# A scan kernel on one core: Exp and Ln from one named table set, state sums two units behind, steps at other places, slot targets turned

## The chip, the core and the metric

One core of a Trainium2 chip. The metric is the device time of one execution in microseconds. The kernel is one hand-scheduled program: every engine runs its own instruction list in order, and semaphores are the only tie between them.

## The reference, cut

A vision tower over 64 images: 196 patches of 768 values and a class token make 197 tokens of 192 channels. One state-space layer, then a mixture of 8 experts:

```python
h = concat(cls_tok, patches @ W.T + b)
# layer 1 on layernorm(h)
xi, z = split(xn @ W_in); xc = silu(conv1d(xi, 4 taps) + conv_b)
Bm, Cm = split(xc @ W_x); delta = softplus(xc @ W_dt + b_dt)
s_t = exp(delta_t * A) * s_t-1 + (delta_t * x_t) * B_t   # 384 channels x 16 states, 197 steps
y_t = sum_states(s_t * C_t) + D * xc
h = h + layernorm((y * silu(z)) @ W_out) * gamma + beta
# layer 2: route each token of layernorm(h) to its best of 8 experts, with a capacity
h = h + prob_max * (expert(x) if kept else x)
```

## The kernel before, in words

**Pairs and units.** The main stage works on 32 pairs of images (`PAIRS`), 394 time steps side by side. A pair's scan is cut into 12 units (`UNITS`: 3 blocks of 128 channels, 4 groups of 4 states); a unit's states fill one of `BUFS` = 5 buffers `hb`. Each engine has a function `body(i, r, on)` with the pair's steps written out at places: k = 0 to 23 (two per unit) on VectorE and ScalarE, u = 0 to 11 on GpSimd and TensorE. `on` tells which neighbours of pair i have steps there: pair i scans (0), i+1 is being projected (1), i+2 is embedded (2), i-1 and i-2 are finished (-1, -2).

**Who does what.** Per unit, ScalarE writes two halves of `exp(delta*A)` into PSUM (`decays`, L703; two buffers, so `decays(k)` waits for scan k-2). VectorE makes `bx` (L1408) and two scans (L1419) in place. GpSimd multiplies by C (`times_c`, L514) and makes `bx` itself for units 5 and 9 (L521). TensorE spreads B for the next unit (`spread_b`, L1039; one bank, free when `bx` is done) and sums states (`state_sum`, L1050 and L1054), `LAG` = 3 units behind the scan. `take_y` (L1426) gates the sums of one block on VectorE.

Around it, for the other pairs: token product (`tok`, L986), `embed` (L1383) and `front_stats`, `front_norm` (L710), transposes (`front_t`, L996; copies L750 to L752), three `conv` products (L1005, L1007; copied at L771), `silu_x` (L800), `bc` and three `dt` products (L1014, L1023; copied at L776 to L783), the softplus (ScalarE: `Exp` L808, two roundings, `Ln` L822; GpSimd: `softplus_sum` L588, `softplus_rest` L594, `make_delta` L599, `make_du` L604), the z products and `silu_z` (L804), B and C split in three bf16 parts (`rest_bc` L527, `middle_bc` L792, `last_bc` L531, `third_bc` L796), C spread and copied (L1043, L757), then `out_product` (L1066), `copy_out` (L722), `out_squares` (L731), `rstd_out`, `out_norm`, `apply_gamma`, `add_residual` (L541, L547), `row_stats` (VectorE, k=1), `rstd` (GpSimd, u=0), `row_norm` (L710 too, ScalarE, k=3), `back_t`, `router`, `take_logits`.

**SyncE** issues the DMAs of body i in this order: patches of pair i+2 (L420), deltas of pair i, block 2 (L442), store of pair i+1's deltas (L433), their blocks 0 and 1, and last `store_rows(i-1)` (L427, L428), which waits for `row_norm(i-1)`. So the patches of pair i+2 are issued after `row_norm(i-2)`.

**Banks.** `ps_k2` are two PSUM banks through which all small products of a pair go in turn; `K_OF`, `OUT`, `TOKS`, `FT`, `BT`, `CS`, `ROUTE` give each product's number in that turn, and a product waits for the copy of the one two before it.

**Slot stage**, after the pairs: rank and target slot of each token (VectorE), then a product of one-hot matrices that turns targets into token ids by slot. 128 columns of 99 tokens go in 16 groups of 8: VectorE makes `lo_hot` (L1557) and 4 columns of `hi_hot` (L1561, L1563), ScalarE 4 (L924, L930, L931), TensorE multiplies (L1254). Then the expert tiles run, unchanged here.

**Table sets.** ScalarE's functions come in sets; a load (ACT_TABLE_LOAD) stands where the active set lacks the next function. In the text below a place is named by its k or u, and a pair's zero is the start of its second `bx`, `bx(1)`.

Of the kernel before, what the change touches and what calls it, by code (L numbers as in the profile page):

```python
# [19 lines left out]
I32 = mybir.dt.int32  # L20
BF16 = mybir.dt.bfloat16
U32 = mybir.dt.uint32
ALU = mybir.AluOpType
# [4 lines left out]
P = 128  # L28
# [6 lines left out]
H0 = 99  # L35
# [20 lines left out]
CLEARED = 6  # L56
# [4 lines left out]
GROUP = 8  # L61
GROUPS = COLS // GROUP
BY_DVE = GROUP // 2
# [9 lines left out]
LAG = 3  # L73
# [5 lines left out]
S_CONSTS = R_CONSTS + 11 + CLEARED  # L79
# [12 lines left out]
def build(nc, x, cls_tok, tok_w, tok_b, w_inx, w_zlo, w_zhi, conv_w, conv_b, w_x, w_dt, b_dt, a_log, d_skip, w_out, gamma,  # L92
# [4 lines left out]
    with ExitStack() as ctx:  # L97
# [95 lines left out]
        at[0] = ob_at  # L193
        assert CLEARED * 4 * DIM <= at[0]
        lo_hot = [carve(H0, GROUP, P) for _ in range(2)]
        hi_hot = [carve(H0, GROUP, 2, SC) for _ in range(2)]
# [9 lines left out]
        exv, prob, rsum, vmax, absent, rank_t, destf, dlo, dhi, idw, iota, one_cols, dhin, probn, idp = (carve(H0, COLS) for _ in range(15))  # L206
        hot_abs = [carve(H0, GROUP - BY_DVE, SC) for _ in range(2)]
        desti, dlo_i, dhi_i = (carve(H0, COLS).bitcast(I32) for _ in range(3))
# [49 lines left out]
        ps_s = pb[5]  # L258
        ps_t = pb[7]
# [86 lines left out]
        s_hotid = sem("ids_by_one_hot_ready")  # L346
        s_hotabs = sem("one_hot_distances_ready")
# [29 lines left out]
        K_OF = (20, 22, 21, 0, 2, 3, 1, 11, 15, 12)  # L377
        MADE = (1, 3, 2, 4, 6, 7, 5, 8, 10, 9)
        TAKEN = (1, 3, 2, 4, 6, 7, 5, 8, 10, 9)
        OUT, TOKS, FT = (4, 9), (6, 7), (16, 17)  # L380
        BT, CS, ROUTE = (13, 14), (8, 10, 18, 5), 19
# [101 lines left out]
        def _(pool):  # L483
# [80 lines left out]
            def slot_consts():  # L564
# [3 lines left out]
                pool.iota(idw.rearrange("p (b f) -> p b f", f=2), [[L, IMAGES], [HSTEP, 2]], base=-NOBODY, channel_multiplier=1,  # L568
                          allow_small_or_imprecise_dtypes=True).then_inc(s_pool1, 1)
                pool.iota(idp.rearrange("p (b f) -> p b f", f=2), [[-L, IMAGES], [-HSTEP, 2]], base=NOBODY, channel_multiplier=-1,  # L570
# [35 lines left out]
            def body(i, r, on):  # L606
                o = 1 - r
                for u in range(UNITS):
                    if 1 in on and u == 2:
                        rest_bc(i + 1, o)  # L610
# [4 lines left out]
                    if -1 in on and u == 8:  # L615
                        rstd_out(i - 1)
                    if -1 in on and u == 10:
                        apply_gamma(i - 1)
# [8 lines left out]
                    if 1 in on and u == 2:  # L627
                        last_bc(i + 1, o)
                    if 1 in on and u == 3:
                        softplus_sum(i + 1)  # L630
# [1099 lines left out]
```

## Time and profile before

| | us |
|---|---|
| median of 3 runs | 2980.11 (2979.86 to 2989.61) |
| the profiled execution | 2973.0 |
| its span | 2971.3 |
| busy: TensorE, VectorE, ScalarE, GpSimd | 2483.1, 2292.0, 2095.8, 2346.7 |
| mean granted TensorE clock | 0.938 of full |

Busy time is a union of an engine's instructions and says nothing about which of them is waited for. The span has three stages: the pairs until about 2300 us, routing and slots until about 2447, the expert tiles until the end. Each stage has its own bound, so the rows are read by stage.

### The profile page before, as it was taken

To read this page: it belongs to the slowest core of one execution; us is meant where nothing else is said; L and a number is where in the kernel's file an instruction comes from. 1 tells how busy PE (TensorE), PEld (TensorE's weight loads), DVE (VectorE), ACT (ScalarE), POOL (GpSimd) and SP (SyncE) were. 2 spreads that over 40 slices of the span, in tenths; PEclk is the share of its full clock that TensorE was granted. 3 is DMA by queue.
4 is the path that set the end of the run, shared out by engine and by line. 5 is a ranking of instruction groups with operands and counts; after the bars stand their busy time and mean duration, and the time that the engine had idled before them with its cause. 6 is when DMAs were issued, how large, how long until landed. Compare 5 with 4: busy or idle time off the path is not lost.

```text
span 2971.3 us, 38064 instructions
## 1 busy us (share of the span) xinstructions
PE 2483.1 (84%) x12650; PEld 1565.3 (53%) x12650; DVE 2292.0 (77%) x2419; ACT 2095.8 (71%) x4267; POOL 2346.7 (79%) x1323
## 2 busy tenths in 40 slices
PE   5788888888888888888888888888875378999997
PEld 3444445444444454444444444544431267888886
DVE  1399999999999999999999999999999475222222
ACT  0678888888888888888888888888875183433432
POOL 0399999999999999999999999999998204644442
PEclk8999999999999999999999999999986599999999
DMA  3444455544445544455544455445541024766652
GB/s 99 98 98 107 121 119 124 123 107 107 107 115 127 120 111 107 120 121 124 122 107 107 109 132 124 108 107 123 122 107 42 16 74 156 240 212 206 216 187 91
DMA packets 165467, 361.11 MB, mean 122 GB/s; under 512 B 18353, under 2 KB 89593, under 8 KB 157848
## 3 DMA queue, kind: packets, MB, share of 16 engines
q1 hardware_dynamic: 152504, 329.59, 44.1%
q0 software_dynamic: 12768, 29.08, 3.0%
q8 instruction: 103, 1.69, 0.3%
q14 instruction: 92, 0.75, 0.1%
HBM read 293.86 MB, written 69.30 MB: 122 GB/s over the span
## 4 chain that ended last, share of the span: by engine, by line
PE 42%; DVE 22%; ACT 16%; DMA 9%; issue 8%; POOL 1%; SPq 1%; DVEq 0%; ACTq 0%; POOLq 0%
DVE arena L1419 12%; DMA arena<-in_x 9%; PE banks L986 8%; PE banks L1318 8%; DVE arena L1408 6%; PE banks L1005 6%; PE banks L1297 5%; ACT banks L703 5%; PE banks L1054 4%; ACT arena L710 3%; PE banks L1305 3%; PE banks L1007 2%; PE banks L1066 2%; ACT L703 1%; DVE arena L1426 1%
## 5 line engine op out<-in xcount | busy, mean ns | idle before, releaser
L1419 DVE TENSOR_TENSOR_SCAN arena<-banks,arena 128x788 f32<-128x788 f32 x768 | 1342.0, 1786 | 98.2 <-ACT banks L703 65.3
L514 POOL TENSOR_TENSOR arena<-arena 128x1576 f32<-128x1576 f32 x384 | 1249.1, 3261 | 25.7 <-DVE arena L1419 25.7
L703 ACT ACTIVATE banks<-arena,neg_a 128x392 f32<-128x392 f32 x1536 | 840.8, 582 | 293.8 <-DVE arena L1419 284.2
L1408 DVE TENSOR_TENSOR arena<-arena,banks 128x1576 f32<-128x1576 f32 x320 | 568.1, 1775 | 25.1 <-PE banks L1039 24.9
L1054 PE MATMUL banks<-arena,gather_q 128*32 128x394 f32 x3072 | 355.0, 536 | 12.8 <-POOL arena L514 12.8
L986 PE MATMUL banks<-wtok,arena 128*99 128x192 f32 x1536 | 295.7, 359 | 66.5 <-DMA arena<-in_x 61.7
L986 PEld LDWEIGHTS banks<-wtok,arena 128*99 128x99 f32 x1536 | 279.4, 186 | 81.1 <-issue 73.4
L666 POOL DMA_INDIRECT out_tokens<-arena x114 | 115.4, 1012 | 243.5 <-DVE arena L1614 223.4
L1005 PE MATMUL banks<-arena,v_lo 128*128 128x394 f32 x768 | 305.0, 542 | 2.2 <-ACT arena L752 1.3
L1599 DVE TENSOR_TENSOR arena<-banks,arena 128x384 f32<-128x384 f32 x57 | 31.8, 558 | 346.6 <-PE banks L1318 346.6
L1023 PE MATMUL banks<-arena,wdt 128*128 128x394 f32 x576 | 213.2, 506 | 33.6 <-ACT arena L777 33.6
L1005 PEld LDWEIGHTS banks<-arena,v_lo 128*128 128x128 f32 x768 | 149.9, 206 | 166.0 <-issue 67.8
L944 ACT ACTIVATE arena<-banks 128x256 f32<-128x256 f32 x57 | 22.0, 385 | 303.8 <-PE banks L1284 303.8
L658 POOL DMA_INDIRECT arena<-rows_scratch,arena x114 | 118.5, 1039 | 145.4 <-DVE arena L1591 110.9
L1318 PE MATMUL banks<-arena 128*128 128x192 f32 x1368 | 232.5, 326 | 0.7 <-DVE arena L1599 0.7
L1318 PEld LDWEIGHTS banks<-arena 128*128 128x128 f32 x1368 | 221.5, 190 | 1.4 <-DVE arena L1599 1.0
L521 POOL TENSOR_TENSOR arena<-arena 128x1576 f32<-128x1576 f32 x64 | 191.1, 2986 | 13.6 <-PE banks L1054 13.5
L1023 PEld LDWEIGHTS banks<-arena,wdt 128*128 128x128 f32 x576 | 104.7, 190 | 139.4 <-ACT arena L777 55.4
L710 ACT ACTIVATE arena<-arena 99x192 f32<-99x192 f32 x256 | 118.4, 534 | 72.9 <-POOL arena L508 72.9
L1297 PE MATMUL banks<-arena 128*128 128x256 f32 x684 | 159.2, 381 | 4.0 <-ACT arena L946 2.4
L1066 PE MATMUL banks<-wout,arena 128*99 128x192 f32 x768 | 145.1, 341 | 15.6 <-ACT arena L783 10.6
L1054 PEld LDWEIGHTS banks<-arena,gather_q 128*32 128x32 f32 x3072 | 62.3, 111 | 168.1 <-issue 137.4
(229 smaller groups left out, 4242.7 us busy)
## 6 DMA issues: line engine op xcount, KB each, us to landing
arena<-delta_du_scratch SPq DMA_DIRECT2D x384, 394.0 KB, 10.5
arena<-in_w_pack SPq DMA_DIRECT2D x57, 1155.0 KB, 5.3
delta_du_scratch<-arena SPq DMA_DIRECT2D x96, 394.0 KB, 3.4
arena<-in_x SPq DMA_DIRECT2D x32, 1176.0 KB, 11.9
rows_scratch<-arena SPq DMA_DIRECT2D x32, 297.0 KB
rows_scratch<-arena SPq DMA_DIRECT2D x32, 294.0 KB
arena<-in_b SPq DMA_DIRECT2D x57, 96.0 KB, 5.3
arena<-in_conv_w SPq DMA_DIRECT2D x1, 2304.0 KB, 9.6
```

The lines of the kernel that those rows point to most:

```text
L514: pool.tensor_tensor(v[:, :, :], v[:, :, :], c_rep[r][:, u % NG].unsqueeze(1).to_broadcast([P, NQ, N2]), ALU.mult).then_inc(s_mulp, 1)
L703: ins = act.activation(o, d, ACT.Exp, scale=neg_a[:, c:c + 1])
L710: ins = act.activation(dst(c), src(c), ACT.Identity, scale=rs[:, c:c + 1], bias=nb[:, c:c + 1])
L986: mm = pe.matmul(v[0:H0, f * DIM:(f + 1) * DIM], patches[:, c, b, f * HSTEP:f * HSTEP + H0], wtok[:, c, :], start=(c == 0), stop=(c == KP ...
L1005: pe.matmul(v[:, 0:N2], v_lo[:, k, c], t_lo[:, :, k:k + L], start=(k == 0), stop=False)
L1023: mm = pe.matmul(v[:, 0:N2], wdt[:, k, c], xz[r][:, k, :], start=(k == 0), stop=(k == MB - 1))
L1054: mm = pe.matmul(ps_y[q * 32:(q + 1) * 32, 0:N2], gather_q[:, :], hb[(UNITS * n + u) % BUFS][:, q, :], start=False, stop=(g == NG - 1), sk ...
L1066: mm = pe.matmul(v[0:H0, f * DIM:(f + 1) * DIM], y[:, k, c:c + H0], wout[:, k, :], start=(k == 0), stop=(k == MB - 1))
L1297: pe.matmul(hidden_part(k, f), wp[g][:, f * P:(f + 1) * P], x[:, 0, :], start=(f not in (2, 3, 5)), stop=False, skip_group_check=True)
L1318: mm = pe.matmul(ps_out[:, f * DIM:(f + 1) * DIM], hid[k % 2][:, c, f * P:(f + 1) * P], w2[:, c, :], start=(c == 0), stop=(c == KF - 1))
L1408: dve.tensor_tensor(hb[(UNITS * n + u) % BUFS][:, :, :], rep[m][:, :, 1, :], ps_b[:, 0:N2].unsqueeze(1).to_broadcast([P, NQ, N2]), ALU.mul ...
L1419: dve.tensor_tensor_scan(v, decay[k % 2], v, 0.0, ALU.mult, ALU.add).then_inc(s_scan, 1)
```

## The change

- ScalarE: a named set with Exp and Ln is loaded explicitly at the start, after `silu_x` and after `silu_z`.
- `LAG` 3 becomes 2; on every engine steps stand at other places, with the banks' turns to match. `silu_z` goes from k=1 to k=13, `add_residual` to the next body's u=0, `embed` from k=10 and 11 to k=9 and 10, the `dt` products ahead of `bc`. SyncE's body is the same.
- Slot stage: targets, probabilities and ids are transposed first; 99 columns of 128 tokens in 11 groups of 9, of which VectorE makes 6 in three wide operations and ScalarE 3. `CLEARED` 6 becomes 5.

```diff
-CLEARED = 6
+CLEARED = 5
-GROUP = 8
-GROUPS = COLS // GROUP
-BY_DVE = GROUP // 2
+GROUP = 9
+GROUPS = H0 // GROUP
+BY_DVE = 6
-LAG = 3
+LAG = 2
...
@@ gpsimd body
+                    if -2 in on and u == 0:
+                        add_residual(i - 2, r)
+                    if 1 in on and u == 3:
+                        softplus_sum(i + 1)
...
-                    if 0 in on and u == 6:
+                    if 0 in on and u == 7:
                         bx_pool(i, 9)
+                    if 1 in on and u == 8:
+                        rest_bc(i + 1, o)
...
+                    if 1 in on and u == 10:
+                        last_bc(i + 1, o)
                     if -1 in on and u == 10:
-                        add_residual(i - 1, o)
+                        apply_gamma(i - 1)
@@ scalar
+            def exp_ln_tables():
+                act.preload_act_table_set("natural_log_exp_and_others")
...
                     if 1 in on and k == 1:
                         silu_x(i + 1, o)
+                        exp_ln_tables()
+                    if 0 in on and k == 1:
+                        copy_c(i, r, o, 0)
+                    if 0 in on and k == 1:
+                        copy_c(i, r, r, 1)
+                    if 1 in on and k == 3:
+                        copy_product(i + 1, o, r, DT + 1)
+                    if 0 in on and k == 3:
                         keep_b(i)
                     if -2 in on and k == 3:
                         row_norm(i - 2, r)
                     if 1 in on and k == 3:
+                        copy_product(i + 1, o, r, DT + 2)
+                    if 1 in on and k == 4:
+                        copy_product(i + 1, o, r, DT)
+                    if 1 in on and k == 4:
+                        softplus_exp(i + 1)
...
+                    if 1 in on and k == 9:
                         softplus_ln(i + 1)
+                    if -2 in on and k == 12:
+                        copy_back_t(i - 2, r, 1)
                     if 1 in on and k == 12:
+                        copy_product(i + 1, o, r, Z)
+                    if 0 in on and k == 13:
+                        silu_z(i, r)
+                        exp_ln_tables()
                     if -1 in on and k == 13:
                         copy_out(i - 1, r, 1)
-                    if -1 in on and k == 14:
+                    if -1 in on and k == 13:
                         out_squares(i - 1, o)
...
+                    if 2 in on and k == 15:
                         front_norm(i + 2, r)
...
+                    if 1 in on and k == 22:
+                        middle_bc(i + 1, o)
+                    if 2 in on and k == 22:
+                        copy_product(i + 2, r, r, 2)
+                    if 2 in on and k == 22:
+                        copy_product(i + 2, r, r, 1)
+                    if 1 in on and k == 23:
+                        third_bc(i + 1, o)
@@ tensor body: dt products at u=0, bc at 1, back_t at 2 and 4,
@@ tok at 3, z at 4, 5, 6, out_product at 2 and 5, router at 6
+                    if 2 in on and u == 8:
+                        conv(i + 2, r, r, 2)
+                    if 2 in on and u == 9:
+                        conv(i + 2, r, r, 1)
+                    if 2 in on and u == 10:
+                        pe.wait_ge(s_gev, 10 * (i + 2) + 1)
+                        conv(i + 2, r, r, 0)
@@ vector body
-                    if -1 in on and k == 5:
+                    if -1 in on and k == 3:
                         take_y(i - 1, o, 2)
+                    if 2 in on and k == 9:
+                        embed(i + 2, r, r, 0)
                     if 2 in on and k == 10:
                         embed(i + 2, r, r, 1)
-                    if 0 in on and k == 13:
+                    if 0 in on and k == 12:
                         take_y(i, r, 0)
-                    if 0 in on and k == 22:
+                    if 0 in on and k == 19:
                         take_y(i, r, 1)
@@ vector, slots
-                for j in range(BY_DVE):
...
+                link(dve.tensor_tensor(hot_same[t % 2], iota..., dhi..., ALU.is_equal))
+                dve.tensor_tensor(v[:, 0:BY_DVE, 0, :], hot_same[t % 2], idp..., ALU.mult)
+                ins = dve.tensor_tensor(v[:, 0:BY_DVE, 1, :], hot_same[t % 2], probc..., ALU.mult)
```

## Rows read from the trace of the kernel before

**Rows 1.** Windows view, 500 to 2000 us: busy time (x instructions) of PE, PEld, DVE, ACT, POOL.
```profile
500.00:2000.00 1500.00, 1283.23 (x6411) 725.82 (x6413) 1408.48 (x1228) 1255.82 (x2440) 1439.63 (x726) 0.96 0.50 116
```

**Rows 2.** Waits, 500 to 2000 us: who waited for whom, us, times, longest.
```profile
PE banks L986 <- DMA arena<-in_x: 50.0, 22, 3.3
DVE arena L1419 <- ACT banks L703: 43.5, 32, 1.7
POOL arena L527 <- ACT arena L777: 26.0, 22, 2.3
DVE arena L1383 <- PE banks L986: 17.2, 20, 1.6
```

**Rows 3.** Timeline of VectorE (DVE): start us, us, engine, line, operation, count.
```profile
400.96 1.76 DVE L1408 TENSOR_TENSOR arena<-arena,banks 128x1576 f32<-128x1576 f32 x1
...
1018.71 1.76 DVE L1408 TENSOR_TENSOR arena<-arena,banks 128x1576 f32<-128x1576 f32 x1
...
1025.53 1.77 DVE L1408 TENSOR_TENSOR arena<-arena,banks 128x1576 f32<-128x1576 f32 x1
1027.40 3.49 DVE L1419 TENSOR_TENSOR_SCAN arena<-banks,arena 128x788 f32<-128x788 f32 x2
1030.81 0.54 DVE L1426 TENSOR_TENSOR arena<-arena,banks 128x394 f32<-128x394 f32 x1
...
1047.72 0.56 DVE L1383 TENSOR_TENSOR arena<-banks,tok_bias 99x384 f32<-99x384 f32 x1 [0.63 <-PE banks L986]
...
1087.77 1.76 DVE L1408 TENSOR_TENSOR arena<-arena,banks 128x1576 f32<-128x1576 f32 x1
...
1701.69 1.76 DVE L1408 TENSOR_TENSOR arena<-arena,banks 128x1576 f32<-128x1576 f32 x1
...
1728.49 0.53 DVE L1383 TENSOR_TENSOR arena<-banks,tok_bias 99x384 f32<-99x384 f32 x1
...
1768.52 1.76 DVE L1408 TENSOR_TENSOR arena<-arena,banks 128x1576 f32<-128x1576 f32 x1
...
2175.66 1.77 DVE L1408 TENSOR_TENSOR arena<-arena,banks 128x1576 f32<-128x1576 f32 x1
```

**Rows 4.** Timelines of ScalarE, the DMA issues (SPq) and TensorE: the patch load's path.
```profile
1023.43 1.85 ACT L710 ACTIVATE arena<-arena 99x192 f32<-99x192 f32 x4
...
1026.08 0.79 SPq L420 DMA_DIRECT2D arena<-in_x  x1
...
1038.16 9.53 PE L986 MATMUL banks<-wtok,arena 128*99 128x192 f32 x48 [2.22 <-DMA arena<-in_x]
...
1719.20 8.01 PE L986 MATMUL banks<-wtok,arena 128*99 128x192 f32 x48 [1.78 <-DMA arena<-in_x]
```

**Rows 5.** Groups of table loads, 500 to 2000 us (busy us, mean ns), then ScalarE's timeline.
```profile
L703 ACT ACT_TABLE_LOAD x44 | 56.5, 1283 | 0.8
L804 ACT ACT_TABLE_LOAD x22 | 28.2, 1283 | 0.4
L822 ACT ACT_TABLE_LOAD x22 | 28.2, 1283 | 0.4
...
1044.40 1.28 ACT L822 ACT_TABLE_LOAD   x1
1045.70 1.19 ACT L822 ACTIVATE arena<-arena 128x1182 f32<-128x1182 f32 x1
```

**Rows 6.** Timelines of ScalarE, VectorE and TensorE in the slot stage.
```profile
2400.78 1.22 ACT L924 ACTIVATE arena<-arena 99x114 f32<-99x114 f32 x4
...
2405.03 1.22 ACT L924 ACTIVATE arena<-arena 99x114 f32<-99x114 f32 x4
...
2400.13 1.23 DVE L1557 TENSOR_TENSOR arena<-arena 99x1024 f32<-99x1024 f32 x1 [1.03 <-PE banks L1254]
2401.27 0.33 DVE L1561 TENSOR_SCALAR arena<-arena 99x114 f32<-99x114 f32 x1
...
2401.02 3.32 PE L1254 MATMUL banks<-arena 99*128 99x228 f32 x16 [0.93 <-ACT arena L931]
```

More of the change, by code:

```diff
@@ L191, in build @@
         mo_end = at[0]
[L193 to L196, printed above, removed]
+        at[0] = CLEARED * 4 * DIM
+        assert at[0] <= ob_at
+        lo_hot = [carve(P, GROUP, P) for _ in range(2)]
+        hi_hot = [carve(P, GROUP, 2, SC) for _ in range(2)]
         assert at[0] <= spv_at, (at[0], spv_at)
@@ L205, in build @@
         assert at[0] >= mo_end, (at[0], mo_end)
-        exv, prob, rsum, vmax, absent, rank_t, destf, dlo, dhi, idw, iota, one_cols, dhin, probn, idp = (carve(H0, COLS) for _ in range(15))
-        hot_abs = [carve(H0, GROUP - BY_DVE, SC) for _ in range(2)]
-        desti, dlo_i, dhi_i = (carve(H0, COLS).bitcast(I32) for _ in range(3))
+        exv, prob, rsum, vmax, absent, rank_t, destf, one_cols, token = (carve(H0, COLS) for _ in range(9))
+        iota = carve(P, P)
+        dlo, dhi, dhin, probc, probn, idp, idn = (carve(P, H0) for _ in range(7))
+        hot_abs = [carve(P, GROUP - BY_DVE, SC) for _ in range(2)]
+        hot_same = [carve(P, BY_DVE, SC) for _ in range(2)]
+        desti, dlo_i, dhi_i = (carve(P, H0 + 1)[:, 0:H0].bitcast(I32) for _ in range(3))
         weights8 = carve(H0, E)
@@ L258, in build @@
         ps_s = pb[5]
+        ps_dest = pb[6]
+        ps_tokens = pb[7]
         ps_t = pb[7]
@@ L1144, in body @@
                         tok(i + 2, r, 1)
-                    if 1 in on and u == 5:
+                    if 1 in on and u == 4:
                         if 2 in on:
@@ L1186, in body @@
                         back_t(i - 2, r, r, 1)
-                    if 1 in on and u == 7:
-                        if -2 in on:
+                    if -1 in on and u == 5:
+                        if 1 in on:
+                            pe.wait_ge(s_gev, 10 * (i + 1) + 8)
+                        else:
+                            pe.wait_ge(s_trb_copied, 2 * (i - 2) + 1)
+                        out_product(i - 1, r, 1)
+                    if 1 in on and u == 5:
+                        if -2 in on:
+                            pe.wait_ge(s_trb_copied, 2 * (i - 2) + 2)
+                        else:
+                            pe.wait_ge(s_h, 2 * (i + 2) + 2)
+                        z(i + 1, o, r, Z + 2)
+                    if -2 in on and u == 6:
+                        if -1 in on:
+                            pe.wait_ge(s_oev, 2 * (i - 1) + 2)
+                        else:
                             pe.wait_ge(s_trb_copied, 2 * (i - 2) + 1)
-                        else:
-                            pe.wait_ge(s_gev, 10 * (i + 1) + 8)
+                        router(i - 2, r)
+                    if 1 in on and u == 6:
+                        pe.wait_ge(s_gev, 10 * (i + 1) + 9)
                         z(i + 1, o, r, Z + 1)
@@ L1249, in _ @@
             pe.matmul(ps_s[:, 0:E], first, tile_end, start=True, stop=True).then_inc(s_endp, 1)
+            pe.wait_ge(s_dest, 1)
+            pe.transpose(ps_dest[:, 0:H0], destf, ident[0:H0, 0:H0])
+            pe.transpose(ps_tokens[:, 0:H0], prob, ident[0:H0, 0:H0])
+            pe.transpose(ps_tokens[:, H0:2 * H0], token, ident[0:H0, 0:H0]).then_inc(s_turned, 1)
             for t in range(GROUPS):
```

255 lines of the change are left out of this document (106 added, 149 removed).

## The prediction

> **What bounds the kernel now.** I read the windows first. Over 1500 us of the scan stage [rows 1] GpSimd is busy 1439.6 us and VectorE 1408.5, so neither has 7% to give. 22 image pairs fall in that stretch, 68.2 us each, of which GpSimd works 65.4. The first and last of 26 steady pairs (400.96 and 2175.66, both the second `bx` of a pair, which I take as a pair's zero) say 68.26 us [rows 3]. Then the waits [rows 2]: per pair VectorE loses 2.0 us to ScalarE's decays (43.5/22) and 0.8 to the token product (17.2/22), TensorE 2.3 to the patches (50.0/22). ScalarE, busy 1255.8 us, has slack.
>
> The timelines show that these are one loop. In the pair from 1018.71 [rows 3] `row_norm` ends at +6.6 (1023.43+1.85 [rows 4]). Only then does SyncE, which has `store_rows` ahead of it in program order, issue the patch load (1026.08). The patches land 12 us later, and the two token products run from 1038.16 for 9.53 us, to +29. `embed` 1 starts there (1047.72 [rows 3]); 40.05 us of uninterrupted VectorE work lead to the next zero at 1087.77. Where the token products end in time the loop is VectorE's own: 1701.69, embed at 1728.49 (+26.8), next zero 1768.52, a pair of 66.8 us with 40.0 behind the embed. So the period is the start of `embed` 1 plus the VectorE work behind it.
>
> The token products take either 8.01 us, all at the full granted clock of 2.4 GHz, or 9.5 to 9.7 where TensorE had stood over 2 us for the patches and the records then show 1.2 GHz for part of them [rows 4]. By the trace the longer form is the usual one: 22 of 27 pairs from 332 us on.
>
> **Part 1, tables.** Before, a pair makes four loads: 44 at L703, 22 at L804, 22 at L822 for 22 pairs, 1.283 us each [rows 5]. `silu_z` and `silu_x` share one visit, `Ln` makes another. The named set removes the `Ln` visit, but `silu_z` moves from k=1 to k=13 and so makes a visit of its own: 2+2 loads again, 5.1 us of ScalarE both times. Gain in load time: nothing. What changes is the place. The stop at k=1 shrinks by one Silu (1.19). At k=13 ScalarE needs decays 1.03, load 1.28, Silu 1.19, load 1.28, copy 0.4, squares 1.4, in all 6.6 us until `decays(14)`; VectorE meanwhile does `bx` 1.87, a scan 1.70, `take_y` 0.46, a scan, `bx` (steps between starts, [rows 3]): 7.6. Hidden, with 1.0 us to spare; that cover is a rival's subject. The Trainium skill ("ScalarE: Activation LUTs", What ACT_TABLE_LOAD costs) adds about 1.38 us of drain to each 1.283 us load. By that figure the stop at k=13 would be 9.4 us, 1.8 past its cover. The trace disagrees: the `Ln` behind its load starts 0.02 us after the load's end (1044.40+1.28 and 1045.70 [rows 5]).
>
> **Part 2, the loop above.** `row_norm` stays at k=3 but `keep_b` now stands just ahead of it. With the shorter stop at k=1 ScalarE arrives in time, so `keep_b` waits for `bx(1)` (+1.8), ends +2.2, and `row_norm` (1.85) ends +4.1. It was +5.1 to +6.6, mean 5.4. SyncE's order is untouched: issue +0.8, 12.0 to the first token product (mean of the steady pairs, 11.3 to 12.9), so +16.9. TensorE is there earlier (about +15, after `back_t` and its copy), so the patches still decide, after about as long a standstill; I take 9.4 us, the mean of the two forms by their frequency. The token products end at +26.3, about 1.7 us earlier than the mean now (+28.0).
> But `embed` 1 moves from behind scan 11 to behind scan 10. That puts 1.70 us more behind it: 40.0+1.7 = 41.7. VectorE itself would be there at +23.8, so it waits 2.4 us. Period: 26.3+41.7 = 68.0, plus 0.3 I allow `decays(17)`, which now has `front_norm`, three products' copies and both transposes' copies ahead of it within two scans: 68.3. Against 68.26: nothing, and 30 times nothing. The lag, the `Ln` loads and the waits at k=2 and k=8 that vanish are swallowed by the one wait that remains.
> Bounds for this term: below, VectorE's floor, 23.8+41.7 = 65.5 a pair, -83 us in all; above, +1.2 a pair, +36 (rival 3).
>
> **Part 3, lag, ring and GpSimd.** Lag 2 on five buffers lets `bx(u)`, which needs the sum of u-5, find it one unit sooner, but TensorE then waits for `times_c(u-2)` in front of `spread_b(u+2)`. GpSimd works 65.4 a pair, under a period of 68, so it follows by less than a unit; cost nothing. If GpSimd fell back by a unit (3.3 us) VectorE would stall at `bx`. `rest_bc` leaves the place where GpSimd waited for its input, 1.2 us a pair (26.0/22 [rows 2]), which was not the bound. `add_residual` goes from u=10 to the next u=0, ahead of `times_c(11)` and of `row_stats`: 1.8 us moved, done before VectorE gets there. `last_bc`, now behind `middle_bc` at k=22, and the three conv copies put `spread_b(0)` 0.5 us ahead of its `bx(0)`: nothing, narrowly.
>
> **Part 4, slot targets.** Groups of 8 columns over 99 partitions become 11 groups of 9 over 128. Now ScalarE bounds a group: 2400.78 to 2405.03, 4.25 us [rows 6], times 16, plus the closing product (3.3) and 1.9 for a start in which TensorE has half its clock: 73.2. After: ScalarE makes 3 columns, 3x0.31+6x0.375 = 3.2. TensorE 3.32x9/8 = 3.7. VectorE: `lo_hot` of 1152 elements, 1.23x1152/1024 = 1.4, and three operations of 684 elements, each about 0.88 by interpolation between 0.33 (114) and 1.23 (1024); less overlap 3.85. VectorE bounds: 11x3.85 = 42.4, plus the tile arithmetic that stands between its groups 1 and 2 and had been cover (3.1), plus the closing product 3.7: 49.2. New ahead of it: three transposes, four ScalarE copies and the conversions, 3.2 against 1.65. Sum: 52.4 against 74.9, -22.4. Bounds: -17 (VectorE 4.4 a group) and -24 (TensorE bounds).
>
> **Part 5, ends.** Drain: `out_product(31, 1)` now stands behind `back_t(30)` and its copies instead of running through behind `out_product(31, 0)`; the chain through the squares starts 2 us later: +2 (0 to +4). Head: the delta path loses a load and the B/C product ahead of it (-3), `spread_b(0)` gets the third conv ahead of it (+4.2): +1 (-4 to +5). The named load at the start replaces one.
>
> **Sum.** 0 - 22.4 + 2 + 1 = -19. The profiled execution took 2973.0 (span 2971.3 and 1.7 around it), which gives 2954 there; the median of the runs shown stands 7 above the profiled one, so 2980.1 - 19 = 2961.
>
> **Rivals.** (2) *The loop shortens.* If TensorE's standstill gets short enough to keep its full clock, the token products take 8.0: embed at +24.9, period 66.9 with the same 0.3, -1.3 a pair, -39, sum -58: 2922. For it: TensorE has more work between +13 and +17; five pairs already run so. Against: 22 do not.
> (3) *ScalarE's second Silu stop becomes the wait.* Place: `decays(14)`, with `take_y(0)` ahead of it needing `silu_z`. It decides from 1.0 us of lateness, every further one is VectorE's. `copy_out(1)` in that stop waits for an output product that now comes after the token products, and `decays(13)` for a Z copy with 0.2 us to spare. Late by 2.2: +1.2 a pair, +36-19: 2997. Against: the output product should end 2.7 us before its copy. Hidden time at each load would do the same: were a load to cost twice its row, the stop grows by 2.6, 1.6 past the cover, +48 and 3009; the 0.02 us gap leaves that 0.02 of this rival's chance. The drain that the Trainium skill (same section) puts at a load is such a mechanism.
> (4) *The named set is not kept*, and `Ln` and the decay behind it load again: 2.6 us of ScalarE at k=9, where VectorE waits 2.4 for the patches anyway: 0 to +18, 2961 to 2979.
>
> **Chances.** Forecast 0.50, with its own range 2940 to 2982 (slot bounds, ends, half a microsecond a pair); (2) 0.28; (3) 0.16; (4) 0.06. About 0.5% (15 us) is what a measurement of this kernel tells from no change. Faster by more: 0.31 of the forecast, all of (2), 0.02 of (4), 0.61. Within: 0.17+0.05+0.03 = 0.25. Slower: 0.02+0.11+0.01 = 0.14. The range 2915 to 2990 takes in most of (2), down to 1.5 a pair, and the milder half of (3), and leaves out some 0.08 on either side.
>
> **What would show it.** Right: four loads a pair, none at `Ln`; `row_norm` ending near +4; VectorE waiting for the token product at `embed` 1 in nearly every pair, 2 to 2.5 us, and hardly for decays; period 68.0 to 68.5; slot groups of 3.9 us bound by VectorE. Wrong: the wait at `embed` 1 under 1 us with a period under 67.3 (2); waits for decays or `take_y` at k=12 to 17 over 1 us (3); six loads (4); slot groups over 4.4 us.

## The result, and the profile after

| | before | changed |
|---|---|---|
| median, us | 2984.86 (2979.86 to 2994.32, 4 runs) | 3021.28 (3011.82 to 3033.83, 4 runs) |
| the profiled execution | 2973.0 | 3011.82 |
| its span | 2971.3 | 3010.1 |
| mean granted TensorE clock | 0.938 | 0.932 |

The ratio is 1.0123, with an interval of 1.0099 to 1.0147: slower by about 1.2%. The forecast was 2961, faster, and the range ended at 2990.

To see where it went I cut both spans at the same marks: the start of the first `bx(1)`, the start of the last `bx` of the last pair, the end of the addition that gives every token its target slot (`destf`, the ranks added to the experts' bases), the end of the last slot product. The pairs thus count 31 periods and the rest of pair 31. In us:

| kernel | head | pairs | drain | slots | experts | span |
|---|---|---|---|---|---|---|
| before | 131.2 | 2163.0 | 77.7 | 74.8 | 524.5 | 2971.3 |
| changed | 132.6 | 2217.4 | 73.8 | 51.1 | 535.2 | 3010.1 |
| difference | +1.4 | +54.4 | -3.9 | -23.7 | +10.7 | +38.8 |
| forecast | +1 | 0 | +2 | -22.4 | 0 | -19 |

The slot stage did what it was to do. The pairs lost more than twice as much. The expert stage is the same code in both; over the executions profiled in this study it took 524 to 551 us, with 545.1 and 548.9 in two kernels whose pairs and schedule differ little from before, so its 10.7 is not put down to the change. On the whole, the longer the stage, the lower TensorE's granted clock in it (windows view: 0.98 at 524.5 us in before, 0.95 at 551.4 in e6); what lowers it is open.

The windows view of the changed kernel, 500 to 2000 us (busy us of TensorE, its weight loads, VectorE, ScalarE, GpSimd), answers to [rows 1]:

```profile
500.00:2000.00 1500.00, 1268.94 (x6267) 714.95 (x6267) 1373.68 (x1200) 1214.99 (x2371) 1402.36 (x706) 0.95 0.48 113
```

VectorE fell from 1408.5 to 1373.7 busy, GpSimd from 1439.6 to 1402.4: every engine does less in the same time, so a wait grew. The waits view of the same stretch (who waited for whom, us, times, longest) names it; it answers to [rows 2]:

```profile
DVE arena L1454 <- PE banks L1073: 60.2, 26, 3.7
PE banks L1042 <- ACT arena L768: 51.2, 21, 2.5
ACT arena L793 <- PE banks L1042: 33.4, 21, 2.0
PE banks L1005 <- DMA arena<-in_x: 38.2, 21, 2.9
DVE arena L1411 <- PE banks L1005: 24.9, 26, 1.6
```

The decays no longer hold up VectorE by much (L1447 waits 9.1 us for L714 in the same view; 43.5 us before). A new line leads: `take_y` (L1454) waits for the state sum (L1073), 60.2 us in 26 waits. The sum itself stands behind the `dt` products (L1042), and these wait for ScalarE's copy of C (L768). VectorE's timeline of one steady pair shows the place. It answers to [rows 3]; the `bx` rows are the first and the last zero of the 26 pairs and the two zeros of the pair shown:

```profile
408.68 1.76 DVE L1436 TENSOR_TENSOR arena<-arena,banks 128x1576 f32<-128x1576 f32 x1
...
1042.78 1.76 DVE L1436 TENSOR_TENSOR arena<-arena,banks 128x1576 f32<-128x1576 f32 x1
1044.65 3.49 DVE L1447 TENSOR_TENSOR_SCAN arena<-banks,arena 128x788 f32<-128x788 f32 x2
1050.64 0.56 DVE L1454 TENSOR_TENSOR arena<-arena,banks 128x394 f32<-128x394 f32 x1 [2.50 <-PE banks L1073]
...
1071.34 0.56 DVE L1411 TENSOR_TENSOR arena<-banks,tok_bias 99x384 f32<-99x384 f32 x1 [1.57 <-PE banks L1005]
...
1114.47 1.76 DVE L1436 TENSOR_TENSOR arena<-arena,banks 128x1576 f32<-128x1576 f32 x1
...
2231.75 1.76 DVE L1436 TENSOR_TENSOR arena<-arena,banks 128x1576 f32<-128x1576 f32 x1
```

From 408.68 to 2231.75 are 26 pairs of 70.12 us; before it was 68.26. In the pair shown `take_y` of block 2 stands still for 2.50 us, at +7.9, and `embed` 1 starts at +28.6 after another wait. Over the 26 pairs VectorE's waits (gaps over 0.15 us) are, per pair:

| | scan k=2 | `take_y(2)` k=3 | scan k=8 | embeds | later | sum |
|---|---|---|---|---|---|---|
| before | 0.46 | 0 | 1.45 | 0.78 | 0.15 | 2.84 |
| changed | 0 | 2.62 | 0 | 1.04 | 0.65 | 4.31 |

Period less waits is 65.4 and 65.8 us, near the 65.5 that the forecast took as VectorE's floor. The two waits that the forecast called "swallowed" did vanish, 1.91 us, and one that it had not listed took their place, 2.62. The rest came at the embeds and later in the pair.

ScalarE's timeline, answering to [rows 4], shows what stands in front of that sum:

```profile
1036.22 1.09 ACT L714 ACTIVATE banks<-arena,neg_a 128x392 f32<-128x392 f32 x2
1037.34 1.28 ACT L811 ACT_TABLE_LOAD   x1
1038.63 1.19 ACT L811 ACTIVATE arena<-arena 128x1182 f32<-128x1182 f32 x1
1039.84 1.28 ACT L701 ACT_TABLE_LOAD   x1
1041.13 0.89 ACT L768 ACTIVATE arena<-banks 128x394 f32<-128x394 f32 x2
...
1045.67 0.59 ACT L793 ACTIVATE arena<-banks,bdt 128x394 f32<-128x394 f32 x1 [1.64 <-PE banks L1042]
...
1047.01 1.86 ACT L721 ACTIVATE arena<-arena 99x192 f32<-99x192 f32 x4
```

TensorE's timeline of the same time, down to the token products:

```profile
1038.09 0.87 PE L1073 MATMUL banks<-arena,gather_q 128*32 128x394 f32 x8
...
1041.68 7.92 PE L1042 MATMUL banks<-arena,wdt 128*128 128x394 f32 x18 [2.45 <-ACT arena L768]
...
1049.70 0.87 PE L1073 MATMUL banks<-arena,gather_q 128*32 128x394 f32 x8
...
1061.60 9.70 PE L1005 MATMUL banks<-wtok,arena 128*99 128x192 f32 x48 [1.95 <-DMA arena<-in_x]
```

And the patch load among SyncE's issues:

```profile
1049.66 0.75 SPq L428 DMA_DIRECT2D arena<-in_x  x1
```

The first `dt` product waits until C's first spread has been copied out of the bank it is to write (L768). The copy stands on ScalarE behind `silu_x` and its two table loads, 3.8 us. So TensorE stands still for 2.45 us, then runs three `dt` products in one piece (18 matmuls, 7.92 us). I call the standstill and this piece the wall. The last state sum of the pair before (1049.70) comes behind it, and VectorE is ready for its result at 1048.14 (1044.65+3.49).

The windows view shows the clock inside that wall (the third number from the end is the granted clock):

```profile
1040.00:1041.60 1.60, 0.00 (x0) 0.00 (x0) 1.60 (x3) 1.59 (x3) 1.60 (x1) 1.00 0.00 0
1041.70:1043.00 1.30, 1.30 (x3) 0.66 (x4) 1.20 (x8) 1.30 (x4) 0.09 (x1) 0.58 0.00 0
1043.00:1045.00 2.00, 2.00 (x5) 1.03 (x4) 1.90 (x2) 1.02 (x3) 1.83 (x5) 0.50 0.00 0
1045.00:1049.50 4.50, 4.50 (x15) 2.47 (x13) 3.14 (x2) 3.83 (x9) 4.22 (x2) 0.96 0.01 4
```

In this pair TensorE's clock is full while it stands, falls to 0.50 (1.2 GHz) just after it works again, and is back near full from 1045. In all 26 pairs a part of the first `dt` product ran at the low clock; in 20 of them the fall came after the restart, in 6 up to 1.8 us ahead of it. In the mean the first `dt` product starts 3.68 us ahead of the second; with a standstill of 1.15 us, in e2 below, 2.24. The groups view of TensorE gives the mean `dt` matmul as 618 ns; it was 505 before.

```profile
L1042 PE MATMUL banks<-arena,wdt 128*128 128x394 f32 x378 | 170.3, 618 | 51.2 <-ACT arena L768 51.2
```

`row_norm` is behind the same wall: in front of it stands the copy of the second `dt` product (L793, 1.64 us of waiting). It ended at +6.0 on average, not at the +4.1 of the forecast; the patch load followed it (1049.66), the first token product started at +18.8, not +16.9.

The groups of table loads answer to [rows 5]: 43+22+21, 1283 ns each, four a pair, none at `Ln`.

```profile
L701 ACT ACT_TABLE_LOAD x43 | 55.2, 1283 | 0.8
L815 ACT ACT_TABLE_LOAD x22 | 28.2, 1283 | 0.4
L811 ACT ACT_TABLE_LOAD x21 | 26.9, 1283 | 0.4
```

The activation behind a load starts 0.01 us after the load's end (1037.34+1.28, 1038.63), and the load 0.03 us after the decay in front of it (1036.22+1.09, 1037.34). The Trainium skill ("ScalarE: Activation LUTs", What ACT_TABLE_LOAD costs) adds a drain of about 1.38 us to each load; this trace has no room for it on either side, and that of before none between load and activation.

And the slot stage, timelines of VectorE and TensorE, answering to [rows 6]:

```profile
2444.32 1.36 DVE L1585 TENSOR_TENSOR arena<-arena 128x1152 f32<-128x1152 f32 x1
2445.60 0.86 DVE L1589 TENSOR_TENSOR arena<-arena 128x684 f32<-128x684 f32 x1
...
2447.29 0.86 DVE L1592 TENSOR_TENSOR arena<-arena 128x684 f32<-128x684 f32 x1
...
2448.07 1.35 DVE L1585 TENSOR_TENSOR arena<-arena 128x1152 f32<-128x1152 f32 x1
...
2448.21 4.20 PE L1282 MATMUL banks<-arena 128*128 128x228 f32 x19 [0.18 <-DVE arena L1592]
```

A group takes 3.75 us (2444.32 to 2448.07), bound by VectorE, TensorE 0.18 us behind it: as forecast (3.85).

### The profile page after: what moved, and what is told of

It reads as the page before. It is cut to its first block, busy times and chain, and to the rows that moved or that the text cites. A ratio compares the mean times of both kernels' runs of the same rounds, so it can differ in the third digit from the quotient of the medians.

```text
span 3010.1 us, 37757 instructions
## 1 busy us (share of the span) xinstructions
PE 2502.4 (83%) x12595; PEld 1567.5 (52%) x12595; DVE 2291.6 (76%) x2318; ACT 2057.0 (68%) x4176; POOL 2345.6 (78%) x1322
## 4 chain that ended last, share of the span: by engine, by line
PE 40%; ACT 22%; DVE 18%; DMA 9%; issue 8%; POOL 2%; SPq 1%; another core or an unknown queue 0%; DVEq 0%; ACTq 0%; POOLq 0%
DVE arena L1447 9%; DMA arena<-in_x 8%; PE banks L1346 7%; PE banks L1005 7%; PE banks L1042 6%; PE banks L1024 5%; PE banks L1325 5%; ACT banks L714 4%; DVE arena L1436 4%; PE banks L1333 3%; ACT L701 3%; ACT arena L721 2%; PE banks L1026 2%; ACT arena L742 1%; ACT L811 1%
## 5 line engine op out<-in xcount | busy, mean ns | idle before, releaser
L1447 DVE TENSOR_TENSOR_SCAN arena<-banks,arena 128x788 f32<-128x788 f32 x768 | 1347.0, 1786 | 45.5 <-ACT banks L714 13.0
L714 ACT ACTIVATE banks<-arena,neg_a 128x392 f32<-128x392 f32 x1536 | 838.1, 581 | 295.1 <-DVE arena L1447 294.1
L1436 DVE TENSOR_TENSOR arena<-arena,banks 128x1576 f32<-128x1576 f32 x320 | 567.7, 1774 | 26.2 <-PE banks L1058 25.9
L1073 PE MATMUL banks<-arena,gather_q 128*32 128x394 f32 x3072 | 349.4, 528 | 21.1 <-POOL arena L522 21.1
L1024 PE MATMUL banks<-arena,v_lo 128*128 128x394 f32 x768 | 291.4, 523 | 59.4 <-ACT arena L782 41.7
L1042 PE MATMUL banks<-arena,wdt 128*128 128x394 f32 x576 | 258.8, 616 | 79.8 <-ACT arena L768 76.6
L1005 PE MATMUL banks<-wtok,arena 128*99 128x192 f32 x1536 | 279.5, 346 | 54.7 <-DMA arena<-in_x 49.1
L1005 PEld LDWEIGHTS banks<-wtok,arena 128*99 128x99 f32 x1536 | 265.5, 178 | 66.9 <-issue 59.6
L1024 PEld LDWEIGHTS banks<-arena,v_lo 128*128 128x128 f32 x768 | 143.2, 196 | 210.9 <-ACT arena L782 63.0
L1042 PEld LDWEIGHTS banks<-arena,wdt 128*128 128x128 f32 x576 | 134.1, 238 | 192.7 <-ACT arena L768 84.3
L1058 PE MATMUL banks<-arena,pick 128*128 128x394 bf16 x320 | 109.2, 341 | 83.8 <-DVE arena L1436 74.5
L1073 PEld LDWEIGHTS banks<-arena,gather_q 128*32 128x32 f32 x3072 | 61.9, 110 | 179.0 <-issue 137.5
```

The costliest lines, as they stand in the source:

```text
L714: ins = act.activation(o, d, ACT.Exp, scale=neg_a[:, c:c + 1])
L1005: mm = pe.matmul(v[0:H0, f * DIM:(f + 1) * DIM], patches[:, c, b, f * HSTEP:f * HSTEP + H0], wtok[:, c, :], start=(c == 0), stop=(c == KP ...
L1024: pe.matmul(v[:, 0:N2], v_lo[:, k, c], t_lo[:, :, k:k + L], start=(k == 0), stop=False)
L1042: mm = pe.matmul(v[:, 0:N2], wdt[:, k, c], xz[r][:, k, :], start=(k == 0), stop=(k == MB - 1))
L1073: mm = pe.matmul(ps_y[q * 32:(q + 1) * 32, 0:N2], gather_q[:, :], hb[(UNITS * n + u) % BUFS][:, q, :], start=False, stop=(g == NG - 1), sk ...
L1436: dve.tensor_tensor(hb[(UNITS * n + u) % BUFS][:, :, :], rep[m][:, :, 1, :], ps_b[:, 0:N2].unsqueeze(1).to_broadcast([P, NQ, N2]), ALU.mul ...
```

## The experiments

A ratio is against executions of the kernel before taken in the same series; the kernel before had medians of 2969 to 2994 in them, so ratios and periods say more than times. "Period" is the mean of 26 steady pairs of the one profiled execution. Line numbers shift by a few where an edit adds lines. The theories: **the wall** (VectorE loses the wait at `take_y(2)`; V in the texts below), **the loop** (`row_norm`, patch load, token products, `embed` 1 set the period, other waits are only slack in it; L below), and whether these two add, or each hides the other.

**e1, take_y later.** In the changed kernel:

```diff
-                    if -1 in on and k == 3:
+                    if -1 in on and k == 5:
                         take_y(i - 1, o, 2)
```

> The changed kernel with take_y of block 2 back at k=5 of VectorE, nothing else. It waited 2.6 us a pair at k=3 for the state sum behind the three dt products. Theory L (the loop through row_norm, patch load and token products sets the period): that chain does not touch VectorE's take_y, so the wait reappears at embed 1 and the period stays at 70.1 us within 0.4; the time stays within 12 us of the changed kernel's 3021. Theory V (VectorE's own stall is the cost): the period falls by 2 to 2.6 us a pair, 60 to 78 in all, to about 2950.

Measured: 3073.98 us, ratio 1.028 (1.0242 to 1.0318), period 71.55. Both missed, by 50 us and more. The waits moved and grew (waits view, 500 to 2000 us):

```profile
PE banks L1069 <- DVE arena L1454: 81.7, 42, 3.3
PE banks L1042 <- ACT arena L768: 51.2, 21, 2.5
DVE arena L1436 <- PE banks L1058: 38.7, 17, 2.7
```

The wall is untouched (51.2). `bx(2)` (L1436) needs a B spread (L1058) that stands behind the wall on TensorE too, so VectorE stops there a step later. And the first sum of the next block (L1069) waits until `take_y` has emptied its bank: with the sums at lag 2 that bank is wanted a unit earlier, so the old place k=5 now stops TensorE, 81.7 us. With lag 2 the old place costs 1.4 us a pair more. That was run with the wall standing; k=4, or k=5 with the wall gone, was not.

**e2, C's copy first.** In the changed kernel, ScalarE at k=1:

```diff
-                    if 1 in on and k == 1:
-                        silu_x(i + 1, o)
-                        exp_ln_tables()
                     if 0 in on and k == 1:
                         copy_c(i, r, o, 0)
+                    if 1 in on and k == 1:
+                        silu_x(i + 1, o)
                     if 0 in on and k == 1:
                         copy_c(i, r, r, 1)
+                    if 1 in on and k == 1:
+                        exp_ln_tables()
```

> The changed kernel with ScalarE's copy of C group 0 ahead of silu_x and the Exp/Ln load behind the copy of C group 1. The first dt product, which waits for that copy, then starts at the end of silu_x, about 1.7 us sooner, after under 1 us of standing instead of 2.45, and so runs at the full clock (2.0 us, not 3.7). Theory L: row_norm ends near +4.3 instead of +6.1, the token products 1.6 us sooner, the take_y wait disappears, period 68.3 to 68.7, in all -45 to -55: 2970. Theory V: take_y's wait of 2.6 goes and the period falls by as much, 67.5, -78: 2943. Rival C (the dt products keep the half clock wherever they stand): the first stays at 3.5 us or more and the gain is 1.7 a pair at take_y but under 0.5 at row_norm.

Measured: 3005.26 us, ratio 1.0036 (1.0009 to 1.0063), period 69.70: less gained than either theory had it. The `dt` products start 1.3 us earlier and the first takes 2.24 us in the mean instead of 3.68, without the half clock in 23 of 26 pairs, so rival C falls; the wait at `take_y(2)` falls from 2.62 to 0.31 and `row_norm` ends at +4.4, close to the forecast's +4.1. So the wait at `take_y(2)` comes from what stands ahead of C's first copy. The edit does two things, the copy ahead of `silu_x` and the second load behind the copy of group 1; they were not run apart, and the `dt` products now wait for `silu_x` itself (L811, 23.8 us). Yet the pair gains only 0.42 us: 2.9 us a pair now stand at the two embeds. The waits view of e2 says why:

```profile
DVE arena L1412 <- PE banks L1006: 57.9, 37, 3.4
PE banks L1006 <- DMA arena<-in_x: 53.0, 21, 3.7
```

So does its group of token products (busy us, mean ns, idle before):

```profile
L1006 PE MATMUL banks<-wtok,arena 128*99 128x192 f32 x1022 | 207.7, 373 | 53.0 <-DMA arena<-in_x 53.0
```

TensorE, freed earlier, stands longer for the patches (53.0 us against 38.2), and the token products take 9.9 us in the mean instead of 8.8. The start is 1.5 us earlier (+17.3), the end 0.3 (+27.2). This is the forecast's own loop, with 42.4 us behind `embed` 1.

**e3, patches early.** In the changed kernel the patches of pair i+3 are issued in front of `store_rows(i-1)`, those of i+2 no longer:

```diff
-                if 2 in on:
+                if i == -2:
                     load_patches(i + 2)
...
+                if 3 in on:
+                    load_patches(i + 3)
```

> The changed kernel with SyncE issuing the next patch load ahead of store_rows, a body earlier, so it no longer waits for row_norm. Theory L: TensorE does not stand 1.9 us for the patches, the token products start near +16.5 instead of +18.9 and more often at full clock, embed 1 is bound by VectorE's own +26.4 (it still waits at take_y); period 68.5 to 69.0, -35 to -48: 2980. Theory V: the patch load is hidden anyway, under 0.3 us a pair.

Measured: 2993.45 us, ratio 1.0009 (0.999 to 1.0027), period 69.11, 0.1 above the range of the first theory. **e4** is the same edit in the kernel before:

> The kernel before with the same early patch load. Theory L: embed 1 falls to VectorE's own +26.8 in every pair, period 66.8 to 67.0 as in its two undisturbed pairs, 1.3 to 1.45 less, -40 to -45: about 2940. Theory V: under 10 us.

Measured: 2968.93 us, ratio 0.9923 (0.99 to 0.9946), period 67.61: between the two theories. In both the patch wait at the token products is gone, and their matmuls are short (groups view of e4):

```profile
L988 PE MATMUL banks<-wtok,arena 128*99 128x192 f32 x1056 | 175.2, 326 | 0.0
```

The same group in e3:

```profile
L1007 PE MATMUL banks<-wtok,arena 128*99 128x192 f32 x1008 | 174.0, 329 | 2.2
```

366 ns a matmul before, 326 now. The loop was real in both kernels, but worth only 0.65 us a pair in the one and 1.0 in the other: once it is cut, VectorE's other waits stand (in the changed kernel `take_y` at 2.72).

**e5, both edits** (e2 and e3):

> The changed kernel with both edits of e2 and e3: the copy of C group 0 ahead of silu_x, and the patch load a body earlier. e2 took the dt products off VectorE's take_y but left embed 1 waiting 2.9 us in all for the token products; e3 took the patches out of that but kept the take_y wait. If the two are the only stalls of the changed schedule ahead of embed 1 (theory W, two walls in series, each hiding the other), embed 1 starts at VectorE's own +24.2, the 42.4 us behind it stay, and the period is 66.5 to 67.0: some 3.3 us a pair under the changed kernel, 2915 to 2930. If they are independent (theory I), the gains of e2 and e3 add: 70.1-0.4-1.0 = 68.7, 2975.

Measured: 2946.54 us, ratio 0.9866 (0.9841 to 0.989), period 67.70: between the two theories, as new waits came behind `embed` 1 (0.42 us a pair at a `bx`, 0.59 at a scan). The gains alone were 0.42 and 1.01, together they are 2.42: each wait had covered part of the other. The kernel is faster than before from here on; its pairs are level with those of e4 (67.61), the old schedule with the same patch order.

**e6, embed later.** In the changed kernel `embed` 0 and 1 go back to k=10 and 11, `front_stats` to 11:

```diff
-                    if 2 in on and k == 9:
+                    if 2 in on and k == 10:
                         embed(i + 2, r, r, 0)
-                    if 2 in on and k == 10:
+                    if 2 in on and k == 11:
                         embed(i + 2, r, r, 1)
-                    if 2 in on and k == 10:
+                    if 2 in on and k == 11:
                         front_stats(i + 2, r)
```

> The changed kernel with embed 0, embed 1 and front_stats back at k=10, 11 and 11. The token products still end near +27.6, but scan 11 now stands ahead of that wait instead of behind it. Theory E (the earlier place of embed cost what it could not use): embed 1 is reached at +28.1 by VectorE itself, the work behind it falls from 42.5 to 40.8, period 68.8 to 69.1, -30 to -40: about 2985. Rival F: everything behind embed 1 is bound by ScalarE or TensorE, and the period stays within 0.3 of 70.1.

Measured: 3005.26 us, ratio 1.0044 (1.0023 to 1.0065), period 69.66: between the theory and its rival. `embed` 1 starts 0.6 later and 1.0 less stands behind it. The forecast's +1.70 for moving a scan behind `embed` 1 was thus part of the loss: 0.46 a pair come back.

**e7, the named set alone**, in the kernel before: a load of the named set at the start and after `silu_x`, nothing moved.

```diff
+                    if (1 in on or 0 in on) and k == 1:
+                        act.preload_act_table_set("natural_log_exp_and_others")
```

> The kernel before with the named set alone: one explicit load at the start and one behind silu_x, every step at its old place. Two loads a pair instead of four, ScalarE 2.6 us less busy. Theory L (loop): the Ln stop at k=11 lies beside VectorE's wait for the token products, period unchanged within 0.3, time within 10 us of before. Rival S: the loads are on the path, -1.2 a pair or more, -40.

Measured: 2987.39 us, ratio 0.9992 (0.9974 to 1.001), period 68.51. Loads fell from four to two a pair (groups view):

```profile
L805 ACT ACT_TABLE_LOAD x22 | 28.2, 1283 | 0.4
L853 ACT ACT_TABLE_LOAD x22 | 28.2, 1283 | 0.4
```

2.57 us of ScalarE a pair were taken away and nothing came of it here. The stop of VectorE at k=8 stayed at 1.44: it isn't made by the `Ln` load. The Trainium skill ("ScalarE: Activation LUTs", Table sets: the hidden batching unit) advises to batch activations by set; here that does lower the loads, as the rows show, and the time doesn't follow.

**e8, turned slots alone**, in the kernel before (the slot stage's hunks, `GROUP`, `BY_DVE`, `CLEARED`; lag 3 and every pair step as before):

```diff
-CLEARED = 6
+CLEARED = 5
...
-GROUP = 8
-GROUPS = COLS // GROUP
-BY_DVE = GROUP // 2
+GROUP = 9
+GROUPS = H0 // GROUP
+BY_DVE = 6
...
```

> The kernel before with the turned slot stage alone. By the changed kernel's trace the stage takes 51.5 us instead of 74.8: -23. It also shows whether the expert stage grows with it (535 against 524.5 us from the last slot product on): if the growth belongs to the earlier slot end or to CLEARED = 5, the gain here is 12 to 14; if it was chance of that execution, 20 to 25.

Measured: 2954.54 us, ratio 0.9883 (0.9862 to 0.9903), period 68.27, slot stage 51.1. The median says -36 where the stage says -23.7; the profiled execution was the slowest of the four (2967.34, its expert stage 545.1), the other three 2952.2 to 2954.6. So the gain is larger than the 20 to 25 expected. The profiled execution does not show where the 12 us beyond the slot stage are: its pairs are as before, and its expert stage is longer.

**e9, the schedule of before with all that does not need the lag**: the edits of e8, e7 and e4 together.

> The schedule of before with lag 3, plus turned slots, plus the named set, plus the patches of pair i+3 issued ahead of store_rows(i-1). Theory 'terms add': slots -35 and patches -23 by their own runs, the named set nothing, since the stop of 1.4 us at k=8 stood with and without the Ln load: period 67.6, time near 2928, ratio 0.981. Rival 'the Ln load had only been hidden by the loop over the patches': with the loop out of the way the named set now pays up to 1.4 us a pair: period 66.3, time near 2888, ratio 0.967.

Measured: 2925.26 us, ratio 0.9856 (0.9823 to 0.989), period 67.25. The time is that of the first theory; the ratio is a little higher, as the kernel before took 2969 in that series. The stop at k=8 stayed at 1.45 here too, against the rival. The period is 0.36 below that of e4, from which the pairs differ by the named set alone; with one profile each, this is a hint that the set may be worth something once the patches are early, no more.

**e10, lag 2 alone**, in the kernel before:

```diff
-LAG = 3
+LAG = 2
```

> Before with LAG = 2 alone, every step at its place. Theory 'places, not lag': the pair's period stays 68.3 (68.0 to 68.6), the time 2985 +-10, ratio 0.997 to 1.003; the loss of the change then lies in its places. Rival 'the lag costs': TensorE stands for GpSimd's product of unit u-2 ahead of the next spread of B, VectorE stands at bx, half a microsecond or more a pair: 3000 or above, ratio over 1.005.

Measured: 3433.29 us, ratio 1.1559 (1.1521 to 1.1597), period 83.63. The first theory missed by far. The rival's open bound (over 1.005) holds it, but not its mechanism: TensorE waits for VectorE's `take_y`, not for GpSimd. The waits view, 500 to 2000 us:

```profile
PE banks L1050 <- DVE arena L1426: 190.0, 53, 4.6
DVE arena L1419 <- ACT banks L703: 163.4, 72, 5.0
DVE arena L1408 <- issue: 150.6, 37, 7.5
```

VectorE's timeline at one of the stops:

```profile
1029.04 0.54 DVE L1426 TENSOR_TENSOR arena<-arena,banks 128x394 f32<-128x394 f32 x1
...
1037.38 1.80 DVE L1408 TENSOR_TENSOR arena<-arena,banks 128x1576 f32<-128x1576 f32 x1 [6.09 <-issue]
```

And TensorE's at the same time:

```profile
1029.64 1.36 PE L1050 MATMUL banks<-arena,skip 128*128 128x394 f32 x2 [4.25 <-DVE arena L1426]
1030.92 1.54 PE L1054 MATMUL banks<-arena,gather_q 128*32 128x394 f32 x8
...
1036.96 0.33 PE L1039 MATMUL banks<-arena,pick 128*128 128x394 bf16 x1
```

The first sum of a block waits for `take_y` of the block before, which still stands where lag 3 had it. TensorE stops 4.25 us, its next eight sums take 1.54 us where 0.87 is usual, a conv product follows, and only then comes the B spread (L1039, 1036.96) for which VectorE's `bx` has been standing. With all that waits so the pair is 15.4 us longer. So I read the change's earlier places for `take_y` (k=3, 12, 19) as the price of lag 2; lag 2 with these places alone moved was not run. The one at k=3 is where it met the wall.

**e11, all three edits** (e2, e3, e6) in the changed kernel:

> The change with C's copy and the dt products early and the patches early (as in the run of both, ratio 0.987), plus embed at k=10 and 11 as in before. Theory 'nothing waits at embed any more': period 67.7 as in the run of both, ratio 0.987 +-0.002. Rival 'the later place is worth its 0.46 us a pair again': 14 us less, ratio 0.982.

Measured: 2901.36 us (2900.5 to 2902.69), ratio 0.977 (0.9738 to 0.9802), period 66.59. The rival held, and more than held: the later embeds bring 1.1 us a pair here and brought 0.46 in e6. Against e9 of the same series, the old schedule with the new slots, the named set and the patches early, it is 24 us in all and 0.66 us a pair shorter: with these three edits the changed schedule is the better one. VectorE is busy 1444.9 of 1500 us, against 1373.7 in the changed kernel (windows view of e11):

```profile
500.00:2000.00 1500.00, 1312.22 (x6551) 716.45 (x6551) 1444.90 (x1262) 1277.49 (x2502) 1476.57 (x745) 0.97 0.50 120
```

**e12, the same without the first edit** (e3 and e6):

> The change with the patches early and embed at k=10 and 11, but C's copy and the dt products where the change has them (the best run, ratio 0.977 and period 66.6, less its first edit). Theory 'the dt wall costs VectorE by itself': take_y(2) waits 2.7 us at k=3 and nothing later gives it back, period 66.6-0.5+2.7 = 68.8, ratio 0.995 to 1.000. Rival 'the wait at take_y is given back at embed, the C edit is worth nothing once the other two are there': period 66.6 to 67.2, ratio 0.977 to 0.983.

Measured: 2973.28 us, ratio 0.9934 (0.9911 to 0.9956), period 68.25. Between the two, nearer the first (68.8 and 0.995 for it, 67.2 for the rival): the `take_y` wait is back, 2.48 us a pair, and 1.66 us of it show in the period (68.25 for 66.59). Its waits view has it as before the first edit:

```profile
DVE arena L1456 <- PE banks L1075: 55.2, 23, 2.5
```

The periods side by side, for the changed kernel with C's copy first (c), patches early (p), embeds later (e):

| none | c | e | p | p, e | c, p | c, p, e |
|---|---|---|---|---|---|---|
| 70.12 | 69.70 | 69.66 | 69.11 | 68.25 | 67.70 | 66.59 |

Each alone gives 0.4 to 1.0; the three give 3.53, though their sum is 1.89 (c with e alone was not run). Beside the old schedule the table says what C's place costs. With the patches as they were, the change lost 1.86 us a pair (70.12 for 68.26), and c gives back 0.42. With the patches early in both it loses 1.50 (69.11 for 67.61), and c gives back 1.41. That is what two waits in a row on one engine look like: shorten the first and the second takes most of it.

## Why the prediction was wrong

**The sum.** By the stages: pairs +54.4 for 0, drain -3.9 for +2, head +1.4 for +1, slots -23.7 for -22.4, experts +10.7 for 0. The pair term failed; it is 54 of the 58 us between 2954 and the profiled 3011.8.

**The step that failed** is in part 2: "With the shorter stop at k=1 ScalarE arrives in time, so `keep_b` waits for `bx(1)` ..., and `row_norm` ends +4.1". It ended at +6.0. Two of the change's moves were read as harmless and not followed through the queues behind them. The `dt` products had moved ahead of `bc` and in front of the last state sum on TensorE; the copy of the second `dt` product had moved in front of `row_norm` on ScalarE. The forecast named what waits for the patches and for the decays, but not what the first `dt` product waits for: the bank that C's copy, itself behind `silu_x` and two loads, sets free. e2 changes the order of that copy, `silu_x` and the second load alone, and `row_norm` ends at +4.4, the `take_y` wait is 0.31.

**But that step is not the whole miss.** e2 has the forecast's `row_norm`, and its period is 69.70, 1.4 above the forecast. The terms that stay are sized too small: the first token product starts at +17.3 (forecast 16.9), the two products take 9.9 us (forecast 9.4, their mean in before), and 42.4 us stand behind `embed` 1 (forecast 42.0); 0.4+0.5+0.4 are, with rounding, the 1.4. The forecast took the standstill in front to be "about as long" as before. It is 2.6 us a pair for 2.3, and 11 of 26 pairs have products of 10.4 to 11.0 us, where before has one. With the patches early, on the other hand, the copy's place accounts for nearly all of the loss (1.41 of 1.50 us).

**take_y(2)** has no line in the forecast at all, though its move from k=5 to k=3 was part of the change. e1 and e10 show what its old place costs with lag 2, where the bank of block sums is wanted earlier: 1.4 us a pair more in e1.

**Part 3**, on lag, ring and GpSimd ("cost nothing"), was right for the ring and GpSimd, which is on neither new wait. It missed that the lag ties the sums to the places of `take_y`. e10 puts 15.4 us a pair on a lag without its places, and its longest wait is that tie (190.0 us in 53 waits).

**The loop** of part 2 was right as a mechanism: e3 and e4 remove its wait and its slow token products, and e2 makes it bind again. The token products were sized 9.4 and took 8.75 (27.51-18.76), since TensorE stood less; so they ended at +27.5, 1.2 after the forecast, where the start was 1.9 late. The forecast's reading that the long form comes where TensorE had stood over 2 us is only roughly so: in the trace of before four of the 26 pairs have it after 1.8 to 2.0 us, and one has the short form after 2.3. Behind `embed` 1 stood 42.5 us, forecast 42.0. 1.2+0.5, and 0.1 between the product's end and the embed, are the 1.8 that the period (70.12 for 68.3) was off. But the loop's account hid the second wait: in it, a wait ahead of `embed` 1 costs nothing as long as the tokens come later, and the tokens came later through the same wall.

**The loads.** Four a pair and none at `Ln`, as forecast, and their time worth nothing in that schedule, which e7 shows by leaving two of the four out. But the forecast tied the stops at k=2 and k=8 to the decays, and e7 adds that the one at k=8 has nothing to do with the `Ln` load. "Nothing" for load time was right; the place of the load in front of C's copy wasn't costed.

**Slots.** Right in size, in the bounding engine and in the group time (3.75 for 3.85).

**The rivals.** The slower side had 0.14, by way of a stop at `decays(14)` (3). The waits there, `take_y(0)` 0.15 and the scan behind it 0.29 a pair, came, but are not where the time went. So the sign came from a mechanism that no rival named. Rival (2), full clock at the token products, is what e3, e5 and e11 have in every pair (329 ns a matmul in e3), but there it took an edit of SyncE's order. The sets were kept, so (4) fell.

**Not settled:** why the expert stage varies by 25 us between executions of like kernels, what lowers the granted clock in it, and the 12 us in e8 that its slot stage doesn't account for.

## What to carry to other kernels

When a step moves in a hand-ordered queue, ask of every instruction behind it on that engine what it waits for and who waits for it, and of every bank or buffer who must empty it first; here a copy of 0.4 us behind an activation and two table loads held up 8 us of TensorE work and, through it, two other engines. A lag between producer and consumer and the places of the steps that empty the shared banks are one parameter, not two. Where one engine has two waits in a row, an edit tried alone shows little: the three edits here look worth 0.4 to 1.0 us a pair each and are worth 3.5 together.

## What the runs showed of the hardware

A short standstill of TensorE costs more than its length: the granted clock falls to 0.50 around the restart, so the price lies on the first products behind the wait. Behind the 2.45 us in front of the `dt` products a part of the first one ran at the low clock in all 26 pairs (3.68 us to the next, in the mean); behind 1.15 us, in e2, in 3 of 26 (2.24). The fall itself is read mostly after the restart in the changed kernel's wall (20 of 26), and mostly during the standstill at e2's token products (17 of 26).

This makes a shorter wait in front bring less, or nothing: in e2 a start 1.5 us earlier became an end 0.3 us earlier, as TensorE then stood longer and the 48 token matmuls went from 347 to 373 ns. Without the standstill they took 326 to 329.
